# Graph layer with residual norm on one core: two native chunks instead of four, one power for the norm and an older rstd, y normalised in place, one residual slot

## What is computed

```python
mask = incidence_m > 0
head = mask / jnp.maximum(jnp.sqrt(jnp.sum(head * head, axis=-1, keepdims=True)), EPS)
inc = incidence_m + head
edge_fea = inc @ cur
edge_degree = jnp.sum(inc, axis=-1, keepdims=True)
x = _layernorm(x + edge_fea / edge_degree, axis=-1)
```

## Time and profile before

| | us |
|---|---|
| median of 3 executions (lowest, highest) | 425.17 (419.24, 425.68) |
| the profiled execution, its own time | 418.96 |
| its span, first to last instruction | 417.2 |
| PE busy in the span | 390.9 |
| DVE, ACT, POOL busy | 374.3, 372.5, 337.8 |

### The profile page before, as it was taken

One profiled execution on the slowest core, in us unless ns is written; L12 is line 12 of the kernel. 1 busy time (PEld: TensorE's weight loads), 2 busy tenths in 40 slices (PEclk: granted clock), 3 DMA queues, 4 the chain that ended last, 5 costly groups with the idle time before them and its releaser, 6 DMA issues.

```text
span 417.2 us, 8912 instructions
## 1 busy us (share of the span) xinstructions
PE 390.9 (94%) x2190; PEld 345.6 (83%) x2190; DVE 374.3 (90%) x756; ACT 372.5 (89%) x512; POOL 337.8 (81%) x248
## 2 busy tenths in 40 slices
PE   0279999999999999999999999999999999999994
PEld 0268789888888888888888888888888888888884
DVE  0669889999999999999999999999999999999941
ACT  4867699999999999999999999999999999998420
POOL 2210389899999999999999999999999999999860
PEclk9999999999999999999999999999999999999998
DMA  8999996567676666666676666666676666661100
GB/s 232 257 238 253 264 252 199 172 198 219 187 226 207 216 199 196 202 202 193 213 213 193 208 196 195 199 204 195 209 218 191 207 196 196 198 199 42 38 26 14
DMA packets 36175, 79.90 MB, mean 192 GB/s; under 512 B 9536, under 2 KB 17728, under 8 KB 36160
## 3 DMA queue, kind: packets, MB, share of 16 engines
q1 hardware_dynamic: 35776, 78.68, 64.8%
q10 hardware_dynamic: 384, 1.05, 0.9%
HBM read 75.50 MB, written 4.19 MB: 191 GB/s over the span
## 4 chain that ended last, share of the span: by engine, by line
PE 82%; DVE 7%; issue 4%; ACT 3%; POOL 2%; ACTq 1%; POOLq 0%; DVEq 0%
PE edge L996 43%; PE edge L1005 22%; PE edge L951 15%; DVE inc L613 3%; DVE incT L629 2%; POOL inc_split L468 1%; DVE x_split L589 1%; ACT sign_out L234 1%; ACTq L153 1%; ACT scaled L245 1%; PE sums L946 1%; POOL norm L487 1%; PE sums L925 1%; ACT L276 0%; POOL rstd L452 0%
## 5 line engine op out<-in xcount | busy, mean ns | idle before, releaser
L468 POOL TENSOR_TENSOR inc_split<-incT,inc_split 128x896 fp32r<-128x896 f32 x120 | 252.9, 2132 | 5.3 <-DVE incT L629 5.1
L996 PE MATMUL edge<-x_split,inc_split 128*128 128x512 f32 (+1 forms) x870 | 210.2, 393 | 0.0
L996 PEld LDWEIGHTS edge<-x_split,inc_split 128*128 128x128 f32 x870 | 156.9, 188 | 29.5
L613 DVE SCALAR_TENSOR_TENSOR inc<-raw,scaled 128x1024 f32<-128x1024 f32 x128 | 153.5, 1200 | 2.8 <-ACT scaled L245 2.8
L629 DVE STREAM_TRANSPOSE incT<-inc 128x1024 f32<-128x1024 f32 x128 | 155.6, 1226 | 0.3
L245 ACT ACTIVATE scaled<-raw,norm 128x1024 f32<-128x1024 f32 x128 | 141.7, 1109 | 14.4 <-POOL norm L487 9.7
L234 ACT ACTIVATE sign_out<-raw 128x1024 int8<-128x1024 f32 x128 | 133.5, 1043 | 1.9 <-DMA raw<-in_adj_dram 1.9
L1005 PEld LDWEIGHTS edge<-x_split,inc_split 128*128 128x128 f32 x840 | 104.8, 191 | 2.3
L1005 PE MATMUL edge<-x_split,inc_split 128*128 128x256 f32 x840 | 106.0, 283 | 0.0
L256 ACT CAST inc_split<-incT 128x896 fp32r<-128x896 f32 x90 | 82.0, 935 | 5.9 <-DVE incT L629 5.8
L951 PE MATMUL edge<-x_native,incT 128*128 128x256 f32 x256 | 63.5, 389 | 2.5 <-DVE incT L629 2.4
(11 more groups left out here) (35 smaller groups left out, 135.7 us busy)
## 6 DMA issues: line engine op xcount, KB each, us to landing
raw<-in_adj_dram SPq DMA_DIRECT2D x504, 128.0 KB, 2.5
rows<-in_x_dram SPq DMA_DIRECT2D x32, 128.0 KB, 2.4
out_dram<-rows SPq DMA_DIRECT2D x32, 128.0 KB, 2.1
x_stage<-in_x_dram SPq DMA_DIRECT2D x8, 256.0 KB, 10.4
x_stage<-in_x_dram SPq DMA_DIRECT2D x8, 192.0 KB, 12.2
raw<-in_adj_dram ACTq DMA_DIRECT2D x8, 128.0 KB, 4.7
x_native<-in_x_dram SPq DMA_DIRECT2D x4, 128.0 KB, 6.4
```

What stands on the lines that cost most here:

```text
L468: nc.gpsimd.tensor_tensor(lo_of(s, q), incT[:, s, 0:SPLIT, q, :], hi_of(s, q).bitcast(fp32), ALU.subtract).then_inc(lo_by_pool, 1)
L613: nc.vector.scalar_tensor_tensor(inc[:, q, :], raw[:, s, q, :], 0.0, scaled[q % 2][:, :], ALU.is_gt, ALU.add, accum_out=part_sums[:, s, 0, ...
L996: last = nc.tensor.matmul(edge[s][:, c0:c1], inc_split[s][:, 0, b, :, :].rearrange("p q j -> p (q j)"), x_split[:, b, :, :].rearrange("p h ...
```

## The change

`NATIVE` is 2, so 30 chunks of a tile go through the hi and lo products. `EARLY` is 4. `half` and `minus_half` become one row of five powers, and count and variance one row of five values: `norm_of` now makes the tile's four norms and the rstd of the tile four back in one POOL instruction, and `rstd_of` is left for the last four tiles. `y` is normalised in place and stored from there, so `y_first` waits for the store of two tiles back, and the residual has one slot whose load waits for the y before. 21 small matmuls (`warm_up`) stand in PE's order before the first products, and tiles 0 and 1 are interleaved a little. The calls of the first tiles stand in another order on all engines, and tiles 6 to 9 are written out (the loops begin at 10).

```diff
-    NATIVE = 4
+    NATIVE = 2
-    EARLY = 6
+    EARLY = 4
...
             def norm_of(t, s):
                 pool.wait_ge(count_ready, t - EARLY + 1)
-                nc.gpsimd.tensor_tensor(norm[:, s, :], count[:, s, :], half[:, :], ALU.pow).then_inc(norm_ready, 1)
+
+                pool.wait_ge(var_ready, t - 3)
+                nc.gpsimd.tensor_tensor(norm_rstd[:, s, :], count_var[:, s, :], powers[:, :], ALU.pow).then_inc(norm_ready, 1)
...
             def load_residual(t, s, reuse):
                 if reuse:
-                    sp.wait_ge(y_ready, t - 1)
-                sp.dma_start(xres[:, s, :], x_rows[t]).then_inc(xres_in[s], 16)
+                    sp.wait_ge(y_ready, t)
+                sp.dma_start(xres, x_rows[t]).then_inc(xres_in[s], 16)
...
                 for s in range(2):
                     t = 2 * u + s
                     for k in range(G):
                         load_quarter(t, s, k, True)
                     store(t - 5, 1 - s)
-                    load_residual(t - 2, s, True)
+                    load_residual(t - 3, 1 - s, True)
...
             def y_first(t, s, u):
...
-                dve.wait_ge(result_ready, t - 1)
+                dve.wait_ge(stored[s], 16 * u)
...
-            def shift_of(t, s):
-                dve.wait_ge(rstd_ready, t + 1)
+            def shift_of(t, s, alone=0):
+                if alone:
+                    dve.wait_ge(rstd_ready, alone)
+                else:
+                    dve.wait_ge(norm_ready, t + 5 - EARLY)
...
+            def warm_up():
+                nc.tensor.matmul(edge[0][:, D:D + P], quad_sum[:, :], quad_sum[:, :], start=True, stop=True)
```

More of the change, by code:

```diff
@@ L59, in gnn_resnorm_kernel @@
         inc_split = [inc_split0, inc_split1]
[L61 to L64, removed]
+        rows = sb("rows", [P, 3, D], fp32)
+        xres = rows[:, 0, :]
+        y = rows[:, 1:3, :]
         sign_out = sb("sign_out", [P, 2, COLS], mybir.dt.int8)
[L67 to L72, removed]
-        quad_sum = sb("quad_sum", [P, P], fp32)
[L74 to L83, removed]
+        small = sb("small", [P, 68], fp32)
+        part_sums = small[:, 0:16].rearrange("p (s k q) -> p s k q", s=2, k=2)
+        count_var = small[:, 16:26].rearrange("p (s k) -> p s k", s=2)
+        norm_rstd = small[:, 26:36].rearrange("p (s k) -> p s k", s=2)
+        powers = small[:, 36:41]
+        count = count_var[:, :, 0:G]
+        norm = norm_rstd[:, :, 0:G]
+        own_quarter = small[:, 41:45]
+        deg_pick = small[:, 45:49]
+        stats = small[:, 49:55]
+        mean_var = small[:, 55:59].rearrange("p (s k) -> p s k", s=2)
+        shift = small[:, 59:61]
+        table_load = small[:, 61:62]
+        deg = small[:, 62:63]
+        rdeg = small[:, 63:64]
+        stats_seen = small[:, 64:65]
+        quad_sum = sb("quad_sum", [P, P], fp32)
         scaled = [pb(f"scaled{i}", [P, COLS], fp32) for i in range(2)]
@@ L358, in _ @@
             scale_quarter(6, 0, 1)
-            with act.Fori(3, PAIRS - 2) as u:
+            normalise(2, 0)
+            sign_quarter(7, 1, 3, 1)
+            scale_quarter(6, 0, 2)
+            sign_quarter(7, 1, 3, 2)
+            sign_quarter(7, 1, 3, 3)
+            round_quarter(6, 0, 0)
+            scale_quarter(6, 0, 3)
+            sign_quarter(8, 0, 4, 0)
+            round_quarter(6, 0, 2)
+            normalise(3, 1)
+            scale_quarter(7, 1, 0)
+            round_quarter(6, 0, 3)
+            scale_quarter(7, 1, 1)
+            sign_quarter(8, 0, 4, 1)
+            scale_quarter(7, 1, 2)
+            sign_quarter(8, 0, 4, 2)
+            sign_quarter(8, 0, 4, 3)
+            scale_quarter(7, 1, 3)
+            round_quarter(7, 1, 0)
+            sign_quarter(9, 1, 4, 0)
+            round_quarter(7, 1, 2)
+            sign_quarter(9, 1, 4, 1)
+            scale_quarter(8, 0, 0)
+            round_quarter(7, 1, 3)
+            normalise(4, 0)
+            scale_quarter(8, 0, 1)
+            scale_quarter(8, 0, 2)
+            sign_quarter(9, 1, 4, 2)
+            sign_quarter(9, 1, 4, 3)
+            round_quarter(8, 0, 0)
+            scale_quarter(8, 0, 3)
+            sign_quarter(10, 0, 5, 0)
+            round_quarter(8, 0, 2)
+            scale_quarter(9, 1, 0)
+            sign_quarter(10, 0, 5, 1)
+            round_quarter(8, 0, 3)
+            normalise(5, 1)
+            scale_quarter(9, 1, 1)
+            scale_quarter(9, 1, 2)
+            sign_quarter(10, 0, 5, 2)
+            sign_quarter(10, 0, 5, 3)
+            scale_quarter(9, 1, 3)
+            round_quarter(9, 1, 0)
+            sign_quarter(11, 1, 5, 0)
+            scale_quarter(10, 0, 0)
+            scale_quarter(10, 0, 1)
+            round_quarter(9, 1, 2)
+            normalise(6, 0)
+            round_quarter(9, 1, 3)
+            sign_quarter(11, 1, 5, 1)
+            with act.Fori(5, PAIRS - 2) as u:
                 scale_quarter(2 * u, 0, 2)
@@ L486, in norm_early @@
                 pool.wait_ge(early_count, G * t + q + 1)
-                nc.gpsimd.tensor_tensor(norm[:, t % 2, q:q + 1], count[:, t % 2, q:q + 1], half[:, 0:1],
+                nc.gpsimd.tensor_tensor(norm[:, t % 2, q:q + 1], count[:, t % 2, q:q + 1], powers[:, 0:1],
                                         ALU.pow).then_inc(early_norm, 1)
@@ L1033, in _ @@
-            tile(4, 0, {("native", 0): lambda: sum_early(5, 2), ("native", 3): lambda: sum_early(5, 3),
-                        ("hi", 25): lambda: sum_quadrants(4, 0, early=True)})
-            tile(5, 1, {("hi", 18): lambda: sum_quadrants(5, 1, early=True)})
+            warm_up()
+            warm_up()
+            warm_up()
+            warm_up()
+            warm_up()
+            sum_early(1, 2)
+            warm_up()
+            warm_up()
+            warm_up()
+            warm_up()
+            warm_up()
@@ new lines, in _ @@
+            sum_degree(1, 1)
+            tile(2, 0, {("native", 1): lambda: sum_early(3, 2), ("hi", 8): lambda: sum_early(3, 3),
+                        ("lo", 21): lambda: sum_quadrants(2, 0, early=True)}, first=True)
+            tile(3, 1, {("lo", 9): lambda: sum_quadrants(3, 1, early=True)})
+            tile(4, 0, {("hi", 28): lambda: sum_quadrants(4, 0)})
+            tile(5, 1, {("hi", 24): lambda: sum_quadrants(5, 1)})
+            tile(6, 0, {("hi", 24): lambda: sum_quadrants(6, 0)})
```

396 lines of the change are left out of this document (237 added, 159 removed).

## The result

The changed kernel takes 453.41 us at the median (452.65 to 456.29, 6 executions), the kernel before 425.08 (419.24 to 425.68, 6 executions). The ratio is 1.0837, with a 95% interval of 1.0807 to 1.0867: 8.4% slower. All ratios here are taken between undisturbed executions, and those of the kernel before lie at 418 to 420 us, which is why 453.4 counts against about 419 and not against 425; the ratios of runs 1 to 4, 10 and 11 are 0.2 to 0.5% too low, since one of about 424.5 us was counted among them.

What follows compares the result with a forecast made beforehand. PE bound the kernel before; after it, POOL's loop behind the shift's collision would, at 12.75 us a tile. 418.96 + 20.6 (tiles 10 to 29) + 2 (tiles 4 to 9) - 1 (start) = 440.6, so 441 us, range 420 to 449.

Steps and rivals of the forecast that it cites:

- PE binds before, with little room to the others: Kernel before: PE's products set 11.72 us a tile; PE can gain at most about 0.4 before another engine binds.
- The moved shift: DVE's shift, now issued inside POOL's low 1, waits until it ends: 1.4 to 1.8 us instead of 0.74.
- DVE's own loop: DVE's work of 10.7 us a tile plus the longer shift makes its tile 12.1 to 12.5 us.
- POOL waits for shift, normalise and one rounding: After low 1 POOL waits 1.7 us for these, added to its 11.1 of work: a loop of 12.8 us.
- The third loop: ACT's normalise to scaling 3, then DVE's inc 3 to transpose 3: 11.0 us plus the shift itself.
- Tiles 4 to 9: Written-out tiles, where a shift costs 0.1 to 2.2 us: +2 us for all six together, bounds 0 and +6.
- The start: First tiles: warm-up matmuls can save PE about 2 us, but PE waits sooner for signs: -1, bounds -3 and +2.
- The end: Last tiles after the loops: the forecast's sum has no term for them.
- The residual: One slot, loaded behind a store: costs nothing under POOL's longer loop, without that cover up to 0.4 a tile, +8 us.
- The rival of no collision: The shift costs only 0.1 us, all loops stay below 11.56 and PE binds: 412 us, range 409 to 418, chance 0.11.
- The gain of the native chunks: Two native chunks made split save PE 0.16 us a tile, 4.8 us over 30 tiles; lost under the full collision.

Runs made afterwards that it cites:

- run 1: Changed kernel with the shift reading rstd as a per-partition scalar, so one SBUF tensor input, same place: 413.33 us, ratio 0.9834.
- run 2: Changed kernel with PE's quadrant sums at hi chunk 6 instead of 12: 452.08 us, ratio 1.0781.
- run 3: Changed kernel with ACT's sign of quarter 2, two tiles on, moved ahead of normalise: 445.46 us, ratio 1.0597.
- run 4: Changed kernel with the two-input shift moved back behind inc 0 and the next tile's degree on DVE: 456.02 us, ratio 1.0853.
- run 10: Repeat of run 1, the changed kernel with the one-input shift: 413.93 us, ratio 0.9843.
- run 11: Changed kernel with the one-input shift and NATIVE = 4 again, sums of tile 4 at hi chunk 27: 417.03 us, ratio 0.9910.
- run 8: Kernel before the change, with only the shift's rstd given as a per-partition scalar: 419.03 us, ratio 1.0011.
- run 5: Changed kernel with normalise moved behind the two roundings on ACT, two-input shift left in its late place: 440.12 us, ratio 1.0518.
- run 6: Changed kernel with the edits of run 4 and run 5 together: 442.39 us, ratio 1.0543.
- run 7: Run 6 with the residual load issued ahead of the store: 425.92 us, ratio 1.0168.

## Why the prediction was right and wrong

The direction, the cause and the signs that it named were right; the time, 441 with an upper end of 449, was too low by 12.4 us, mostly because one loop was not followed to where it closes.

- *PE binds before, with little room to the others.* Right: runs 8 and 11.
- *The moved shift comes into low 1 and waits it out, 1.4 to 1.8 us where it cost 0.74.* Right: the shift takes 1.84 from its start to the next (1.92 in its row), a little over the range, since it comes 0.35 into low 1 and not 0.45 to 0.66; run 1 shows that the second SBUF tensor makes it wait, and its end with low 1 that it waits for POOL. DVE's own loop was put at 12.1 to 12.5; run 5, where it binds, has 12.68.
- *POOL waits for shift, normalise and one rounding, 1.7 us, its loop 12.8.* Right: 1.61, and 12.8 in run 3, where it alone binds.
- *The third loop is ACT's: normalise, roundings and all to scaling 3, then inc 3 to transpose 3, 11.0 plus the shift.* This is the step that failed. I followed ACT's delay only to DVE's inc 3. The same delay runs through two signs to PE's sums and from there to the count and the norm, and that branch is longer: 13.2 us against POOL's 12.8. The sums' wait for the signs is in the code (`signs_ready` in `sum_quadrants`), and I never laid out what is queued behind normalise on ACT as far as the sums. Runs 2, 3 and 5 show this branch: the sums moved forward only wait longer for the sign, a sign taken out of the branch gives 0.3 to 0.4 us a tile, and normalise taken out of it 0.5. The prediction took the larger of DVE's and POOL's sum, 12.75, where 13.2 was due; 20 tiles by 0.46 are 9.2 of the missing 12.
- *Tiles 4 to 9: +2.* Under-sized: up to the norm of tile 11 run 1 is 4.8 us ahead of the changed kernel (143.90 against 148.71), so the shift alone cost 4.8 there, within the bounds of 0 to +6.
- *The start: -1.* Under-sized the other way: run 1 is 3.1 ahead of the kernel before at that norm (143.90 against 147.04). With four native chunks (run 11, 145.22) it is 1.8, so about 1 of the 3.1 comes from the native chunks of the first tiles, which the prediction had as lost, and the rest is mostly warm-up. That PE would then wait sooner for the signs took little of it back. That the two errors nearly cancel, +1.7 against the +1 predicted, is luck.
- *The end: nothing.* It was put at nothing without a reason and is 2.1: POOL's wait of 1.61 before low 2 goes on in tiles 30 and 31. Run 1, without that wait, takes 36.3 us from the norm of tile 31 to the end, so the shift makes 1.7 of the 2.1.
- *The residual: cost nothing under the longer loops, 0.4 a tile without that cover.* The cover held in the changed kernel (run 4 shows the wait appear as soon as DVE is faster); without it, and in the order of run 6, the load behind the store costs 0.9 a tile and not 0.4, run 6 against run 7.
- *The rival of no collision: 412.* Run 1 is that kernel, at 413.3: the sum without the collision was right to about 1 us. The gain of the native chunks in it was too large by 1.7 (4.8 against 3.1), and that of all the rest slightly too small.

## What to carry to other kernels

In this kernel a DVE instruction with two SBUF tensors cost what was left of POOL's instruction, however small it was itself (0.14 us alone, up to 2.2 behind one of POOL's); so look at its other operand before its place, and give it as a per-partition scalar where it is one. When such an instruction moves, price it by the moment at which it ends and by everything that stands behind its consumers, on every branch until the loop closes, not by the time that its engine loses. An edit that saves a slot ties two queues together, and its cost can lie hidden under another one.

## What the runs showed of the hardware that I had not expected

A one-element `tensor_scalar` with its scalar in SBUF takes 0.17 to 0.22 us while POOL is inside a two-input instruction, where the form with two tensors takes up to 2.2 (run 1 and the changed kernel): the per-partition scalar does not take part in the exclusion. Nor does a second tensor in PSUM: the 128 `inc_quarter` of the changed kernel take 1.17 to 1.23 us each, beside POOL or not. And the first native products of the kernel before took 0.47 us a record where later ones took 0.23, while the granted clock of that stretch reads full (1.00, that is 2.4 GHz) in its windows view; after the warm-up matmuls the first four records took 1.13 together in the changed kernel (second row):

```profile
23.70:27.60 3.90, 3.81 (x9) 3.09 (x10) 3.52 (x7) 0.86 (x1) 0.55 (x1) 1.00 1.08 243
...
23.91 1.13 PE L1075 MATMUL edge<-x_native,incT 128*128 128x256 f32 x4 [1.12 <-DVE incT L687]
```

What held the first ones back is not settled by these runs, since the time of the first matmuls was changed and not the clock.
